# Splitting the shifts of two self attentions on GpSimd instead of VectorE

## The reference

```python
# layer 0: attention without a causal mask, a relative bias added after the softmax
attn = softmax(einsum('bhqd,bhkd->bhqk', q, k) * 128 ** -0.5)      # heads of 8 features
attn = attn + rel_bias_table[i - j + 255].transpose(2, 0, 1)[None]
out = einsum('bhqk,bhkd->bhqd', attn, v); out = norm(out) * ln_gamma + ln_beta
# layer 1: causal attention with a bias that grows linearly with the distance, heads of 4 features
scores = einsum('bhqd,bhkd->bhqk', q, k); scores = where(causal, -inf, scores)
w = softmax((scores + slopes[h] * (j - i)) / 2.0)
out = einsum('bhqk,bhkd->bqhd', w, v).reshape(b, t, 128) @ Wp + bp
```

## Time and profile before

| What | us |
|---|---|
| median of 3 runs | 584.02 |
| lowest, highest | 583.33, 591.06 |
| the profiled execution | 586.47 |
| its span | 584.7 |

### The profile page before, as it was taken

How to read it: one execution, slowest core, us unless ns; L and a number is a source line. 1 busy time by engine, 2 the same in 40 slices (tenths; PEclk the granted TensorE clock), 3 DMA queues, 4 the chain that set the end, 5 groups by cost and what they waited for, 6 DMA issues and landing times.

```text
span 584.7 us, 13038 instructions
## 1 busy us (share of the span) xinstructions
PE 515.5 (88%) x4832; PEld 321.4 (55%) x4842; DVE 425.0 (73%) x1232; ACT 331.8 (57%) x825; POOL 199.0 (34%) x309
## 2 busy tenths in 40 slices
PE   3887888999999999977488997998989989999995
PEld 2532444544455576756344556776667867655543
DVE  7878567254666667588998768753788557798996
ACT  1764435755768879655267573566566644353441
POOL 6940000024365545341345520000224221434774
PEclk9955889999999999999699999999998989999998
DMA  8700000000300000001324833000000000301101
GB/s 291 307 1 4 2 3 4 2 1 0 145 2 1 1 2 3 2 1 34 169 84 135 179 86 101 3 4 2 2 3 3 3 2 2 145 0 67 80 1 36
DMA packets 25889, 27.93 MB, mean 48 GB/s; under 512 B 18249, under 2 KB 22866, under 8 KB 24930
## 3 DMA queue, kind: packets, MB, share of 16 engines
q1 hardware_dynamic: 25826, 27.10, 14.4%
HBM read 22.14 MB, written 4.75 MB: 46 GB/s over the span
## 4 chain that ended last, share of the span: by engine, by line
PE 59%; DVE 19%; issue 8%; ACT 5%; SPq 3%; DMA 2%; POOL 2%; POOLq 0%; DVEq 0%; ACTq 0%
PE B_banks L312 4%; PE A_banks L312 4%; PE A_banks L2108 2%; PE A_banks L248 2%; PE A_banks L1014 2%; PE A_banks L1027 2%; DVE B_moe_h L2075 2%; SPq L276 2%; PE B_banks L248 2%; PE A_banks L1874 1%; DVE A_l0a_nmax L340 1%; PE B_banks L982 1%; PE A_banks L1884 1%; PE B_banks L1035 1%; PE A_banks L1035 1%
## 5 line engine op out<-in xcount | busy, mean ns | idle before, releaser
L2108 PE MATMUL A_banks<-A_moe_xT,w_moe_rows 128*128 128x512 f32 x72 | 36.0, 617 | 1.3 <-DVE A_moe_h L2075 1.3
L832 POOL TENSOR_TENSOR A_l0x_prob<-A_l0x_prob,A_l0x_inverted_sums 128x256 f32<-128x256 f32 (+1 forms) x32 | 25.9, 831 | 28.5 <-DVE A_l0x_inverted_sums L947 28.5
L2108 PE MATMUL B_banks<-B_moe_xT,w_moe_rows 128*128 128x512 f32 x72 | 34.4, 598 | 1.2 <-DVE B_moe_h L2075 1.1
L832 POOL TENSOR_TENSOR B_l0x_prob<-B_l0x_prob,B_l0x_inverted_sums 128x256 f32<-128x256 f32 (+1 forms) x32 | 25.9, 831 | 27.6 <-DVE B_l0x_inverted_sums L947 27.6
L160 POOL TENSOR_TENSOR A_l0a_rstd<-A_l0a_ve,w_const_rows 128x4 f32<-128x4 f32 x2 | 2.0, 1016 | 87.8 <-DVE A_l0a_ve L156 87.8
L379 ACT ACTIVATE A_l0a_expT<-A_banks 128x512 f32<-128x512 f32 x32 | 18.3, 603 | 18.6 <-PE A_banks L327 18.3
L849 ACT ACTIVATE B_l0x_prob<-B_l0x_prob,B_l0x_nmax 128x128 f32<-128x128 f32 x64 | 28.2, 446 | 0.9 <-DVE B_l0x_nmax L929 0.9
L849 ACT ACTIVATE A_l0x_prob<-A_l0x_prob,A_l0x_nmax 128x128 f32<-128x128 f32 x64 | 28.2, 447 | 0.0
L340 DVE TENSOR_REDUCE A_l0a_nmax<-A_banks 128x2 f32<-128x512 f32 x32 | 21.7, 687 | 8.0 <-PE A_banks L248 7.7
L379 ACT ACTIVATE B_l0a_expT<-B_banks 128x512 f32<-128x512 f32 x32 | 18.4, 600 | 15.9 <-PE B_banks L327 15.9
L340 DVE TENSOR_REDUCE B_l0a_nmax<-B_banks 128x2 f32<-128x512 f32 x32 | 21.9, 688 | 7.3 <-PE B_banks L248 7.3
(11 more groups left out here) (602 smaller groups left out, 1598.6 us busy)
## 6 DMA issues: line engine op xcount, KB each, us to landing
w_toeplitz_rows<-in_toeplitz_rows SPq DMA_DIRECT2D x1, 3072.0 KB, 13.1
w_moe_rows<-in_moe_rows SPq DMA_DIRECT2D x1, 2304.0 KB, 8.6
w_l1x_rows<-in_l1x_rows SPq DMA_DIRECT2D x1, 2048.0 KB, 8.4
A_l1x_values<-A_l1a_v_tokens SPq DMA_DIRECT2D x4, 512.0 KB, 2.6
A_l1x_v_groups<-A_l1x_values SPq DMA_DIRECT2D x16, 128.0 KB, 3.3
B_l1x_values<-B_l1a_v_tokens SPq DMA_DIRECT2D x4, 512.0 KB, 3.4
B_l1x_v_groups<-B_l1x_values SPq DMA_DIRECT2D x16, 128.0 KB, 3.3
w_l0x_vo_rows<-in_l0x_vo_rows SPq DMA_DIRECT2D x1, 1024.0 KB, 13.7
```

The costliest lines, as they stand in the source:

```text
L832: ins = pool.tensor_tensor(pair, pair, bcast(rz[:, g % 2, i, :], 2, n), ALU.mult)
L2108: pe.matmul(hidden_bank(k)[:, :], w["moe_w3" if which else "moe_w1"][:, ORDER[i], part, :], xT[:], start=True, stop=True).then_inc(s_h.sem, 1)
```

## The change

In both self attentions the split of the shifts is done by GpSimd. `vector_parts` becomes `gpsimd_parts`: the same four operations (five in `l1a`) on the same tiles. Each step signals a semaphore `s_step` of its own, and the next step waits for it, where before VectorE's common chain was used. The wait for the zeroed tile stands before the first copy into it. On GpSimd the four blocks follow the bias addition in `l0a` and the query splits in `l1a`. The turn strings of all five engines are new. Those of TensorE, ScalarE and SyncE order the same units differently; VectorE's has 30 units fewer in each lane, GpSimd's 36 more.

```diff
--- before.py
+++ after.py
@@ -202,6 +202,7 @@
         self.s_s = st.sem("max_scores_ready", self.BLOCKS * self.JOBS)
         self.s_mx = st.sem("max_done", self.BLOCKS * self.JOBS)
         self.s_parts = st.sem("shift_parts_ready", self.BLOCKS)
+        self.s_step = st.sem("shift_split_steps", (4 if constant is not None else 3) * self.BLOCKS)
         self.s_tp = st.sem("shift_transposed", self.BLOCKS)
         self.s_shT = st.sem("shiftT_ready", self.BLOCKS)
         self.s_e = st.sem("exp_scores_ready", U)
@@ -339,32 +340,45 @@
             out, scores = self.nmax[:, b, c, h:h + n], bank[:, :].rearrange("p (h k) -> p h k", h=n)
         dve.tensor_reduce(out, scores, AX, ALU.max, negate=True).then_inc(self.s_mx.sem, 1)
 
-    def vector_parts(self, dve, link, k):
-
-        dve.wait_ge(*self.s_mx(self.JOBS * (k + 1)))
+    def due_block(self, k):
+
+        return next((n for n in range(U) if self.completed(n) == k), -1)
+
+    def gpsimd_parts(self, pool, k):
+
+        steps = k * (4 if self.constant is not None else 3)
+
+        def after():
+            pool.wait_ge(*self.s_step(steps))
+
+        pool.wait_ge(*self.s_mx(self.JOBS * (k + 1)))
         b, first = k * HB // H, k * HB % H
         src = self.nmax[:, b, :, first:first + HB]
-        if k == 0:
-            dve.wait_ge(*self.s_zero(1))
         if k >= 2:
-            dve.wait_ge(*self.s_tp(k - 1))
+            pool.wait_ge(*self.s_tp(k - 1))
         if self.constant is not None:
-            link.add(dve.tensor_tensor(src, src, self.constant[:, :, first:first + HB], ALU.add))
+            pool.tensor_tensor(src, src, self.constant[:, :, first:first + HB], ALU.add).then_inc(self.s_step.sem, 1)
+            steps += 1
             yield
-            link.wait()
+            after()
         G, n = self.G, HB // self.G
         by_rows = lambda ap: ap.rearrange("p c (a j) -> p c j a", j=G)
         hi, mid, lo = (self.parts[:, k % 2, :, 0:32 * G].rearrange("p c (j x) -> p c j x", j=G)[:, :, :, i * n:(i + 1) * n] for i in range(3))
-        link.add(dve.tensor_copy(hi, by_rows(src)))
+        if k == 0:
+            pool.wait_ge(*self.s_zero(1))
+        pool.tensor_copy(hi, by_rows(src)).then_inc(self.s_step.sem, 1)
+        steps += 1
         yield
-        link.wait()
-        link.add(dve.tensor_tensor(by_rows(self.rest[:]), by_rows(src), hi, ALU.subtract))
+        after()
+        pool.tensor_tensor(by_rows(self.rest[:]), by_rows(src), hi, ALU.subtract).then_inc(self.s_step.sem, 1)
+        steps += 1
         yield
-        link.wait()
-        link.add(dve.tensor_copy(mid, by_rows(self.rest[:])))
+        after()
+        pool.tensor_copy(mid, by_rows(self.rest[:])).then_inc(self.s_step.sem, 1)
+        steps += 1
         yield
-        link.wait()
-        dve.tensor_tensor(lo, by_rows(self.rest[:]), mid, ALU.subtract).then_inc(self.s_parts.sem, 1)
+        after()
+        pool.tensor_tensor(lo, by_rows(self.rest[:]), mid, ALU.subtract).then_inc(self.s_parts.sem, 1)
 
     def vector_shiftT(self, dve, k):
         dve.wait_ge(*self.s_tp(k + 1))
@@ -516,6 +530,9 @@
         pool.wait_ge(*s_stq(TT))
         pool.wait_ge(*s_stk(TT))
         pool.tensor_tensor(xb, x[:], w["beta"][:].unsqueeze(1).broadcast_to([P, TT, D]), ALU.add).then_inc(s_xb.sem, 1)
+        for k in range(a.BLOCKS):
+            yield LOOP + STEP * (a.due_block(k) + 0.9) if k else SCORES + 1.2 * a.JOBS
+            yield from a.gpsimd_parts(pool, k)
         yield LOOP + STEP * (U + 8) + 1.0
         norm2.gpsimd_rstd(pool)
         yield
@@ -589,12 +606,10 @@
                         yield 8.9 + 4.0 * t + 0.5 * (n % 4)
                         copy_stack(dve, dve.tensor_copy, n)
         for u in range(a.first):
-            yield SCORES + 1.2 * u
             if u == a.JOBS:
-                yield from a.vector_parts(dve, link, 0)
                 yield SCORES + 1.2 * u + 1.0
                 a.vector_shiftT(dve, 0)
-                yield SCORES + 1.2 * u + 1.2
+            yield SCORES + 1.2 * u + 1.2 * (u >= a.JOBS)
             a.vector_max(dve, u)
             n = 4 * SB + u
             if n < STEPS and not by_scalar[n]:
@@ -609,9 +624,6 @@
             for i, u in enumerate(range(a.due(n - 1), a.due(n))):
                 yield LOOP + STEP * (n + 0.5 * i)
                 a.vector_max(dve, u)
-            k = a.completed(n)
-            if k is not None:
-                yield from a.vector_parts(dve, link, k)
             if n >= 8 and (n - 8) % Q4 == 0:
                 g = (n - 8) // Q4
                 b2, hg = divmod(g, H // Q4)
@@ -1411,6 +1423,11 @@
                 src = sp_[:, t % 2, part, 0:NQ].rearrange("p (h d) -> p h d", h=H).unsqueeze(2).broadcast_to([P, H, n, DQ])
                 ins = pool.tensor_copy(out, src)
             ins.then_inc(s_stq.sem, 1)
+        for k in range(a.BLOCKS):
+            yield LOOP + STEP * (a.due_block(k) + 0.9) if k else SCORES + 3.0 + 0.75 * a.JOBS
+            if k == 0:
+                pool.wait_ge(*s_rb(2))
+            yield from a.gpsimd_parts(pool, k)
 
     def scalar(act):
         def keys(m):
@@ -1519,13 +1536,10 @@
             ins = dve.tensor_copy(kT[r, j, :], stack_bank(4).bitcast(BF16)[r, :])
         ins.then_inc(s_kT.sem, 1)
         for u in range(a.first):
-            yield SCORES + 3.0 + 0.75 * u
             if u == a.JOBS:
-                dve.wait_ge(*s_rb(2))
-                yield from a.vector_parts(dve, link, 0)
                 yield SCORES + 3.0 + 0.75 * u + 1.0
                 a.vector_shiftT(dve, 0)
-                yield SCORES + 3.0 + 0.75 * u + 1.2
+            yield SCORES + 3.0 + 0.75 * u + 1.2 * (u >= a.JOBS)
             a.vector_max(dve, u)
         for n in range(U + 8):
             yield LOOP + STEP * n
@@ -2409,36 +2420,37 @@
 TURNS = {
     "tensor":
-        "A4 B2 A2 B2 A5 B2 A3 B5 A2 B1 A2 B1 A1 B1 A10 B15 A3 B1 A4 B2 A2 B2 A4 B2 A2 B5 A1 B1 A2 B2 A3 B1 A2 B2 A3 B2 A2 B5 A2 B3 A1 B1 A2 B1 A2 B3 A1 B1 A1 "
...
+        "A4 B3 A2 B1 A5 B2 A3 B4 A1 B1 A2 B2 A2 B1 A3 B3 A1 B1 A2 B1 A4 B6 A1 B4 A2 B1 A4 B2 A3 B1 A1 B1 A1 B1 A3 B6 A2 B1 A2 B2 A2 B1 A2 B2 A2 B1 A1 B1 A2 B2 "
...
     "gpsimd":
-        "B1 A4 B3 A4 B1 A3 B5 A2 B1 A3 B2 A1 B3 A1 B2 A5 B2 A3 B2 A1 B1 A1 B1 A1 B1 A1 B1 A1 B1 A1 B1 A2 B1 A1 B1 A1 B2 A1 B1 A1 B1 A1 B2 A1 B2 A2 B4 A16 B16 "
-        "A3 B3 A3 B1 A1 B1 A1 B1 A1 B1 A2 B2 A3 B2 A2 B2 A1 B1 A7 B1 A2 B3 A1 B2 A1 B5 A2 B4 A1 B2",
+        "B1 A4 B3 A1 B1 A6 B4 A1 B1 A1 B1 A3 B2 A1 B4 A5 B5 A4 B4 A4 B4 A4 B4 A5 B2 A2 B1 A2 B2 A1 B1 A1 B1 A1 B1 A1 B1 A2 B1 A1 B1 A1 B1 A1 B2 A1 B1 A1 B1 A1 "
+        "B2 A1 B1 A1 B1 A1 B4 A16 B9 A5 B7 A5 B5 A5 B5 A5 B10 A3 B3 A3 B1 A2 B1 A1 B1 A1 B1 A1 B2 A2 B1 A1 B1 A1 B1 A1 B1 A2 B1 A5 B1 A3 B2 A1 B2 A1 B2 A1 B4 "
+        "A1 B4 A1 B2",
     "sync":
-        "W3 A1 W1 B1 W9 A1 B1 A1 B1 A1 B1 A1 B1 L2 A7 B1 A1 B2 A1 B3 A1 B3 A1 B1 A1 B2 A2 B2 A1 B1",
+        "W3 A1 W1 B1 W9 A1 B1 A1 B1 A1 B1 A1 B1 L2 A7 B1 A1 B2 A1 B4 A1 B2 A1 B1 A1 B2 A2 B2 A1 B1",
 }
```

## The result

| | kernel before | changed kernel |
|---|---|---|
| median of 20 executions, us | 583.94 | 587.91 |
| lowest, highest | 577.50, 591.06 | 584.21, 591.11 |
| the profiled execution | 586.47 | 588.16 |
| its span | 584.7 | 586.2 |
| granted clock over the span | 0.954 | 0.955 |

The ratio is 1.0099, with a 95% interval of [1.0075, 1.0123]. I had forecast 581.0 in 575.5 to 588.0: the time lies inside the range, at its very end, and on the wrong side of the kernel before.

What follows compares the result with a forecast made beforehand. TensorE was taken as the main bound (busy 515.5 of 584.7 us, 59% of the chain), VectorE second (19%). Terms of -1.5 and -1.4 us sum to -2.9, taking the median from 584.02 to 581.1, forecast 581; range 575.5 to 588.

Steps and rivals of the forecast that it cites:

- The steps' prices and the chain on GpSimd: Split steps: 0.20 us a cast, 0.27 an addition or subtraction; a block's chain 1.18 us in l0a, 1.53 in l1a.
- First attention, -1.5: l0a: TensorE's 0.75 us wait at block 0 goes, lane A's block 1 gives -0.38, lane B's block 2 -0.40.
- the 0.40 taken: l0a, lane B's block 2: of TensorE's 1.46 us idle before the transpose, 0.40 was expected to go.
- The 0.38 for lane A's block 1: l0a: two VectorE split steps between two maxima delay the following maximum; moving them was to gain 0.38 us.
- Second attention, -1.4: l1a: sum of -1.0 for lane A, -0.6 for lane B's start and +0.2 for lane B's block 3.
- -1.0 for lane A's first E: l1a: lane A's block 0 transpose precedes lane B's product, so the first E comes 1.02 us earlier; -1.0 taken.
- the 0.6 taken: l1a: of TensorE's 2.09 us idle before lane B's first E, 0.6 goes, with SyncE's store of t = 3 first.
- The +0.2 for lane B's block 3: End of l1a: exposed chain costs +0.50 on GpSimd, less 0.3 that the new order puts in front.
- The chance for it, 0.03: Rival: the new strings do harm in stages elsewhere than the split; chance 0.03.
- exposed latency: Rival: TensorE's transposes in both attentions wait for GpSimd's longer chain; 587.5 half exposed, 591 to 596 fully; 0.15 to 591, 0.02 beyond 2%.
- The clock rival: First attention: the new order fills a gap and avoids the clock's fall at 32 us; 576.5 us, chance 0.08.
- the trace agrees: Clock rival: the skill says activity releases throttling; the trace was said to agree that a busy TensorE isn't enough, 32 to 34 us.

Runs made afterwards that it cites:

- e3: Split on GpSimd, new order until lane B ends the first self attention, old order behind it, against the kernel before: 582.65 us, 1.0003.
- e1: Split on GpSimd with the old order of units on all five engines, against the kernel before: 583.75 us, 1.0005.
- e8: Split on GpSimd, new order only in the second self attention (l1a), old order elsewhere, against the kernel before: 580.90 us, 0.9974.
- e9: Split on GpSimd, new order only in the second cross attention (l1x), old order elsewhere, against the kernel before: 588.46 us, 1.0100.

## Why the prediction was wrong, by its steps

- **The steps' prices and the chain on GpSimd: right,** 1.05 us for 1.18 in `l0a`. The Trainium skill's ratio of about two for operations with two inputs (GPSIMD Engine Reference, Engine selection) was too high for 16 elements: the traces have 0.220 to 0.249 us against 0.17 to 0.18.
- **First attention, -1.5: the waits went, the time did not.** 0.75 is gone, and of 1.46 nothing is left, more than the 0.40 taken. The 0.38 for lane A's block 1 is a delay that no row shows by itself. Yet e3, the new order in this stage alone, gives 1.0003 [0.9970, 1.0036]. 1.5 us are 0.26 per cent, inside that interval; I can neither claim them nor deny them.
- **Second attention, -1.4: right in part, the size not resolved.** Of its terms the largest, -1.0 for lane A's first E, wasn't earned: the E comes one product earlier, but waits 0.54 us for its DMA, and lane B's last product starts no earlier than before (343.79 and 343.60). Lane B's wait went from 2.09 to 1.21, 0.9 for the 0.6 taken, and its shift is bound by the copy as said; but e1 has 1.4 without the store put first, so most of it isn't due to the store. The +0.2 for lane B's block 3 wasn't paid, and lane A's block 1 has a new wait of 0.68 for GpSimd that I had costed at nothing. e8 gives 0.9974, with 1 inside its interval.
- **"The new strings also reorder units in the stages that the split doesn't touch. They take nothing off and add nothing, and I cost them at 0 with +/-3": this is the step that failed.** One of these stages, `l1x`, costs 1.0100, or 4.9 us by the medians, by itself (e9), as much as the whole loss and more than my +/-3. What the runs show in place of the 0 is more time at half clock in kernels with this order, and, where it could be seen, longer waits of TensorE; the shares of the two are open. I read the new strings where they touch the shifts, and elsewhere counted units instead of asking what each moved unit had been hiding. The diff was there: lane B's first scores ahead of lane A's second transposition, and 38 of TensorE's places, 43 of VectorE's, 33 of ScalarE's and 8 of GpSimd's that hold another unit in this stage.
- **The chance for it, 0.03, was far too small.** A new order of a whole kernel is the larger change of the two, and my rival for a slower kernel was put on the smaller: exposed latency. The three transposes of the changed kernel that wait for GpSimd cost 0.68, 0.24 and 0.23 us, and e1 shows the move at 1.0005. That 587.91 still lies below my 588 is luck: I had drawn that end of the range from the exposed chain, which did not cost it.
- **The clock rival** looked for a gain in the first attention. On the average of kernels the clock does answer to the order, but in another stage and in the other direction. My "the trace agrees" there claims too much: the row shows a busy TensorE at 0.50 from 32 to 34 us, and no activity that releases the clock.

The best of the kernels tried is the move with the new order of `l1a` alone (e8, 580.90 us); at 0.9974 [0.9926, 1.0022] it isn't shown to beat the kernel before, and it is the lowest of many.

## What to carry to other kernels

Where a change comes with a new order of units, price the order stage by stage, the stages that the edit doesn't name as well: for each unit that moves past a wait, ask what now stands in that wait. Test it by cutting the two orders together at a stage's end; nine such kernels found the stage here. Finding the units inside it took four more and did not succeed: one unit moved by one place, in either direction, already changed TensorE's waits around it. And before a gain of 1 us is read from two profiles, look at how far executions of one kernel lie apart.
